# Cross attention of a fused decoder: where the context product, the read of the sums and the context transpose stand in TensorE's and VectorE's order

## The reference

```python
x = layer_norm(x) ; kv_in = concat([x, ctx], axis=1)        # keys: 512 own + 32 of the context
q = x @ Wq ; k, v = split(kv_in @ Wkv)                        # 16 heads of 64
p = softmax(q @ k.T / 8)                                      # per head 512 x 544
x = x + (p @ v) @ Wo
```

## Time and profile before

| | |
|---|---|
| median of 3 runs | 1846.54 us (1839.44 to 1847.07) |
| profiled execution: time, span | 1845.25 us, 1843.4 us |
| granted TensorE clock, mean | 0.957 |
| busy share of the span | PE 90%, PEld 40%, DVE 69%, ACT 52%, POOL 17% |
| cross attention's 128 score steps | from 59.75 us to about 647 us of the span |
| chain that ended last, by engine | PE 75%, DVE 16%, ACT 5%, issue 3%, POOL 1% |

### The profile page before, as it was taken

The page is one execution under the profiler, slowest core; times in us unless marked ns, Lnnn a source line. Parts: engine busy times, 40 slices in busy tenths (PEclk is TensorE's granted clock), DMA queues, the critical chain, the costliest instruction groups (busy, mean ns, idle before and its releaser), DMA issues.

```text
span 1843.4 us, 24921 instructions
## 1 busy us (share of the span) xinstructions
PE 1653.6 (90%) x8074; PEld 736.0 (40%) x8074; DVE 1271.4 (69%) x2994; ACT 949.4 (52%) x2053; POOL 304.5 (17%) x465
## 2 busy tenths in 40 slices
PE   7899999999999989999899988444798899999998
PEld 3355455545544432222244331222443355444443
DVE  7576666767667768888565578999666677762423
ACT  3565556556645516666633566333236366664333
POOL 1000000000001021121277200000000222114443
PEclk9999999999999989999999999777799799999999
DMA  4000000000000220240000000000100512100000
GB/s 193 1 1 1 1 1 1 1 1 1 1 1 21 55 59 23 73 116 2 1 0 1 0 1 1 1 1 1 69 1 1 147 55 73 32 2 1 1 0 23
DMA packets 19806, 44.36 MB, mean 24 GB/s; under 512 B 3872, under 2 KB 13024, under 8 KB 18912
## 3 DMA queue, kind: packets, MB, share of 16 engines
q1 hardware_dynamic: 19200, 42.39, 7.6%
q10 hardware_dynamic: 480, 0.39, 0.1%
HBM read 32.74 MB, written 9.44 MB: 23 GB/s over the span
## 4 chain that ended last, share of the span: by engine, by line
PE 75%; DVE 16%; ACT 5%; issue 3%; POOL 1%; DMA 0%; ACTq 0%; POOLq 0%; SPq 0%; DVEq 0%
PE ps L675 8%; PE ps L639 8%; PE ps L653 6%; PE ps L1226 6%; PE ps L1264 5%; PE ps L1112 5%; PE ps L1699 3%; PE ps L1700 3%; PE ps L596 3%; PE ps L1596 3%; PE ps L1612 3%; PE ps L1707 3%; DVE arena L2063 2%; PE ps L684 2%; DVE arena L2050 2%
## 5 line engine op out<-in xcount | busy, mean ns | idle before, releaser
L1390 DVE TENSOR_REDUCE stat<-ps 128x1 f32<-128x512 f32 (+3 forms) x512 | 279.1, 581 | 86.6 <-PE ps L1116 43.0
L1321 ACT ACTIVATE arena<-ps 128x512 f32<-128x512 f32 (+3 forms) x512 | 247.1, 515 | 154.3 <-PE ps L1264 83.3
L826 DVE TENSOR_REDUCE stat<-ps 128x1 f32<-128x544 f32 x256 | 173.4, 719 | 163.0 <-PE ps L639 163.0
L777 ACT ACTIVATE arena<-ps,stat 128x544 f32<-128x544 f32 x256 | 180.7, 711 | 201.9 <-DVE stat L826 201.9
L1264 PE MATMUL ps<-arena 75*128 75x512 bf16 (+1 forms) x480 | 163.1, 344 | 11.7 <-ACT arena L1321 9.5
L1112 PE MATMUL ps<-arena 72*128 72x128 bf16 (+1 forms) x480 | 163.0, 348 | 8.0 <-DVE stat L1390 7.8
L675 PE MATMUL ps<-arena 128*64 128x512 f32 (+1 forms) x640 | 159.2, 609 | 4.7 <-DVE arena L845 3.3
L639 PE MATMUL ps<-arena 64*128 64x272 f32 x1024 | 152.1, 415 | 5.1 <-ACT arena L777 4.3
L785 ACT COPY arena<-ps 128x512 f32<-128x512 f32 x256 | 137.3, 594 | 15.5 <-PE ps L653 15.5
L653 PEld LDWEIGHTS ps<-wA_sb,arena 128*128 128x128 f32 x1024 | 115.1, 142 | 70.1 <-issue 68.9
L653 PE MATMUL ps<-wA_sb,arena 128*128 128x128 f32 x1024 | 138.3, 278 | 0.0
(11 more groups left out here) (391 smaller groups left out, 2775.2 us busy)
## 6 DMA issues: line engine op xcount, KB each, us to landing
arena<-b_parts SPq DMA_DIRECT2D x180, 96.0 KB
b_parts<-arena SPq DMA_DIRECT2D x64, 128.0 KB, 1.9
reg<-wM_dram SPq DMA_DIRECT2D x1, 3072.0 KB, 10.0
reg<-wB_dram SPq DMA_DIRECT2D x1, 2048.0 KB, 12.4
reg<-wM_dram SPq DMA_DIRECT2D x1, 2048.0 KB, 16.7
reg<-wD_dram SPq DMA_DIRECT2D x1, 1817.0 KB, 10.7
wF_sb<-wF_dram SPq DMA_DIRECT2D x1, 1476.0 KB, 19.8
reg<-b_parts SPq DMA_DIRECT2D x12, 96.0 KB
```

The costliest lines, as they stand in the source:

```text
L777: e.activation(prob_of(P, r).rearrange("p (a k) -> p a k", a=2), score_banks(r), ACT.Exp, bias=x_neg[:, at_:at_ + 1], accum_out=x_sums[:, ...
L826: e.tensor_reduce(x_neg[:, n % 4:n % 4 + 1], score_banks(r), AX.XY, ALU.max, negate=True).then_inc(sem("max_done"), 1)
L1321: e.activation(p_t[:, m % 8, q0:T], ps[:, S1 + m % S2, q0:T], ACT.Exp).then_inc(exp_done, 1)
L1390: e.tensor_reduce(nm[:, G % 2, u // 4, u % 4:u % 4 + 1], ps[:, step % S1, 0:keys(u)], AX.X, ALU.max, negate=True).then_inc(max_done, 1)
```

## The change

Four edits:

1. The context transpose (L658) takes 128 columns of `x_prob` instead of 64 (the added 64 are the second head's first own keys) and writes all 128 partitions of its quarter of bank 6. The reader still takes 64.
2. The context part of the value product, `pv(g, (4,))`, moves from step 4g+9 (between scores and transposes) to the end of step 4g+8, right behind `pv(g, (2, 3))`.
3. On VectorE `pv_read(g)` moves in step 4g+9 from behind the two maxima to ahead of them.
4. SyncE's rows of ones for `a = 1` also wait until GpSimd's split of the narrow attention's second batch is done.

```diff
@@ transposes @@
-                    e.transpose(ps[0:2 * S, 6, q * 128:q * 128 + 128], x_prob[:, P % 3, T:T + 2 * S],
+                    e.transpose(ps[:, 6, q * 128:q * 128 + 128], x_prob[:, P % 3, T:T + 128],
                                 ident).then_inc(sem("ctx_turned"), 1)
@@ b2_pe @@
-                    if r == 1:
-                        if 0 <= (i - 9) // 4 < XP:
-                            pv((i - 9) // 4, (4,))
                     if i == XPAIRS + 5:
                         head_pe(e, range(*HEAD[i]))
...
                     if r == 0 and 0 <= (i - 8) // 4 < XP:
                         pv((i - 8) // 4, (2, 3))
+                        pv((i - 8) // 4, (4,))
@@ b2_dve @@
+                    if r == 1 and 0 <= (i - 9) // 4 < XP:
+                        pv_read((i - 9) // 4)
                     if i < XPAIRS:
                         neg_max(i, 0)
                         neg_max(i, 1)
-                    if r == 1 and 0 <= (i - 9) // 4 < XP:
-                        pv_read((i - 9) // 4)
@@ sp of narrow @@
                             if a and early is not None:
                                 e.wait_ge(sem("pv_done"), XP)
+                                e.wait_ge(split_q, 8)
+                                e.wait_ge(split_k, 8)
```

## The result

The changed kernel takes 1861.07 us (median of 6 runs, 1854.62 to 1869.45) where the kernel before, in the same series, takes 1845.92 (6 runs): ratio 1.0083, 95% interval 1.006 to 1.0107. That is 15.2 us slower, where +14.3 and 1860 were forecast. Its profiled execution took 1860.79 us with a span of 1859.0, 15.6 more than before's 1843.4.

What follows compares the result with a forecast made beforehand. Each step was bound by TensorE's work or a 3.53 us loop through the engines. +30.0 - 3.5 - 19.5 + 5.6 + 1.7 = +14.3 us on 1845.25 gave 1859.6, stated as 1860, range 1850 to 1866.

Steps and rivals of the forecast that it cites:

- The step rule: Cross attention: each step costs the larger of TensorE's work and the 3.53 us loop from scores to next scores.
- The 30.0 added: Step r = 0 of 30 groups: the context product moved there is paid in full, 30 x 1.00 = +30.0 us.
- the 19.5 saved: Step r = 1 of 26 groups: falls only to the loop's 3.53, saving 0.75 each, 19.5 us.
- the three output steps: Step r = 1 of the three groups with `out`, bound by TensorE: 1.17 saved each, 3.5 us in all.
- The moved product's price: Context product in r = 0: taken as 1.00 us, the upper bound, since every change of tile costs about 0.1.
- the lower bound 0.87: Context product in r = 0 without a change of tiles: 0.87 us, total +10.4; a rival given 0.16.
- Q late: Step r = 2: Q waits for ScalarE's copy from bank 7, costing 5.6 us; rival that it is not late, 0.10.
- The early read: VectorE in r = 1: hidden in idle time before the maxima; rival that it pushes them, together +23, chance 0.08.
- The wide transpose: Context transpose: price 0; rival that the narrow one held up the array, 9.0 us less, chance 0.15.
- The end: End of the stage, head steps of the narrow attention: context product delays the first maxima and second product, together +1.7 us.
- The new wait of SyncE: End of the stage: rows of ones issued no later than before despite waiting for the split, price 0.

Runs made afterwards that it cites:

- e7: The changed kernel with the context part of the value product left out, so its sums lack the context: 1827.18 us, ratio 0.9905 to the kernel before.
- e5: The changed kernel with the moved product taking the last block of own keys again in place of the context's: 1854.51 us, ratio 1.0052 to the kernel before.
- e6: The changed kernel with ScalarE copying the values of r = 1 before that step's evacuation, not after: 1862.31 us, ratio 1.0087 to the kernel before.
- e1: The changed kernel with the early read undone, the sums read behind the two maxima of r = 1 again: 1878.39 us, ratio 1.0178 to the kernel before.
- e3: The kernel before with only the early read, ahead of the maxima while the context product stays in r = 1: 1875.39 us, ratio 1.0159.
- e2: The kernel before with only the wide, 128-column context transpose: 1847.55 us, ratio 1.0013.
- e4: The changed kernel with the narrow, 64-column context transpose back: 1859.85 us, ratio 1.0075 to the kernel before.
- e8: The kernel before with VectorE's reads of bank 7 ahead of the maxima in steps r = 2 of groups 26, 28 and 29: 1838.41 us, ratio 0.9969.

## Why the prediction was right

- **The step rule** (TensorE's work or 3.53 us): right in every regular group: r = 0 5.12, r = 1 3.53 with the forecast wait for the exponentials. e7 shows it from the other side. The 30.0 added and the 19.5 saved are as forecast; the three output steps save 1.17 each (6.86 to 5.69).
- **The moved product's price**: 1.00 taken, 1.00 measured. The choice between the bounds rested on the likeness to other changes of tile; e5 shows it to be right, and the lower bound 0.87 is the streaming alone.
- **Q late**: 0.2 with values, 0.3 with a variance forecast; r = 2 grew by 0.20 and 0.30 (4.34 to 4.54 and 4.64). The last group, without K, lost 0.07 and not 0.2. The cause is shown by e6 for the groups with values; for those with a variance it is argued by likeness.
- **The early read**: hidden, by a margin of 0.41 us. Called free in itself; e1 and e3 add that it is a condition of the move, worth 0.75 us a group with it, and a loss of 0.87 a group without it. The prediction gave edit 3 only 0.17; it had assumed the early read when it took r = 1 down to 3.53, and did not say what the move alone would cost.
- **The wide transpose**: 0, shown alone (e2) and behind the move (e4).
- **The end**: +1.7 forecast, -0.49 measured. This term was mis-sized. The first delay of 1.0 came as said, and up to the maxima behind the second product the price is as forecast (1.83 against e3 at a like clock). "From there VectorE sets the pace, so the delay stays" is the step that failed: at the last read the delay was 0.05, and at the end of the stretch 0.4 against e3. The context product no longer stands behind a wait of TensorE for GpSimd (0.54 us before, 1.61 in e3), and the last read waits in VectorE's list and not for its sums. The second product was costed at the low clock that the kernel before met there (0.50 from 668 to 670), and in this execution it ran at 1.00 (680 to 684): its twelve records took the usual 2.94. The rest of the gap to -0.49, about 0.9 us, is the clock of the stretch (0.92 against 0.88).
- **The new wait of SyncE**: not late, but not idle either. It was issued at 685.29, 0.08 after the split's last instruction (682.95 + 2.26 = 685.21), and the sums were ready earlier; so this wait, not `pv_done`, now releases it, 26.7 us after the scores of step 127 where it was 28.5 before. No run has the other edits without this one; that it costs nothing is read from the trace alone.
- **What was not in the sum**: 2.7 us from two steps that met the low clock. It offset the error at the end, so the total is closer than its parts, and that is luck. By the regular steps alone the stage grows by about 12.5, where the terms without the end give 12.6.

## What to carry to other kernels

Work moved between steps is paid by the step that takes it and saved only down to the next bound of the step that gives it: before moving an instruction, write for both steps the length by TensorE and the length by the loop through the other engines. A hidden wait comes back as soon as its cover is shortened, here ScalarE's copy for Q; look for what was slack in the step after. A read out of a shared bank belongs where its data lie ready and its engine idles: the same reordering was a condition of saving 0.75 us a group, a loss of 0.87 a group, or a gain of 1.5 to 2.0 us in each of three steps (beside what the clock gave back); what differed was when the data came.

## What the runs showed of the hardware

- A float32 transpose of 64 columns stands in the array like one of 128: 0.11 us to the next full-width matmul and 0.20 to 0.21 to one on 128 x 64 tiles, with either (e4, before and the changed kernel).
- The change from 128 x 64 to 32 x 64 tiles, two shapes with the same column halves, cost 0.14 us, weight load included (r = 0 of 5.12 us against 4.98 in e5).
- After a wait of TensorE of about 2.1 us the granted clock fell from 1.00 to 0.50 in some executions and not in others: group 28's r = 2 took 6.4 us in two traces (e1, e3; mean clock of the step 1.00), 7.75 to 7.93 in three (before, e2, e5; 0.78 to 0.80) and 8.98 in four (0.64 to 0.65). In e3 it also fell behind a wait of 1.82 us, in group 24 (0.50 from 528 to 530). In the one trace of the kernel without the 2.1 us waits (e8) the stage has no low stretch (1.00).
